# A deeper ring for the streamed halves of a mixture-of-experts combine stage, paid for with single buffers for its two smaller inputs

## The chip, the cores and the metric

The program runs on all 8 cores of one Trainium2 chip. Every core does the whole layer for one of the 8 batch elements (4096 tokens of width 1024); no core waits for another. The metric is the device time of the slowest core, in microseconds.

## The reference, cut to what matters

The layer adds to its input an S4 block and a feed-forward mixture of experts, both computed from the layer-normed input. What the change touches is the second half of the feed-forward part:

```python
h1 = jnp.einsum('td,edi->tei', xf, We1) + be1
h3 = jnp.einsum('td,edi->tei', xf, We3) + be3
h = jax.nn.silu(h1) * h3
yo = jnp.einsum('tei,eid->ted', h, We2) + be2
y = jnp.einsum('te,ted->td', combine, yo)
z = jax.nn.silu(xf @ ws1 + bs1) * (xf @ ws3 + bs3) @ ws2 + bs2
return (y + z).reshape(shape)
```

There are 16 experts of inner width 512 and a shared expert of inner width 1024. `combine` is the routing weight of each token for each expert. All experts are computed densely for all tokens.

## The kernel before, in words

The kernel is written by engine, in phases p0 to p7, with hand-placed semaphores. Each engine's instructions run in the order in which the phases emit them; the order between engines is set by `wait_ge` on semaphores alone. Phases p0 to p5 do the layer norm, the gate, the S4 block and the first half of the experts; p5 leaves silu(h1) in the DRAM tensor `dS` and h3 in `dH`, both bf16 with the inner index as rows and the tokens as columns. `dP` holds the S4 block's output, `dCMBT` the routing weights as 16 rows of 4096 tokens.

Phase p6 (`emit_p6`) is the second half. All second-layer weights stay in SBUF: 16 tiles `w2a[e]`, `ws2b` for the shared expert, and `bep` for the biases. They are loaded at the phase's start by GpSimd DMAs that cast from float32 (L1501, L1505, L1508). The tokens are cut in 16 tiles of 256 (`ts` = 0 to 15), and for each tile the loop runs over 17 steps: e = 0 to 15 for the experts, e = 16 for the shared expert, which is twice as wide. In one step:

- SyncE's queue loads the step's part of `dS` into `sstr[e % 2]` and of `dH` into `hstr[e % 2]` (L1543), 256 KB each, 512 KB each for e = 16. Before it issues them it waits until TensorE has finished the step that used these buffers last, two steps earlier (L1536); across a tile boundary both e = 0 and e = 1 wait for step 16 of the tile before.
- VectorE adds the bias and multiplies the two parts, four instructions of 128x256 (L1613; eight for e = 16), then multiplies all by the routing weights from `cmb6` (L1619; not for e = 16).
- TensorE multiplies the result by the step's weights into a half of PSUM, 32 matmuls of 128x256 (L1595; 64 for e = 16).

After step 16 VectorE adds the bias and the S4 output `abuf` and writes `mtile` (L1628), eight instructions; it does this in its own order before it begins the products of the next tile. GpSimd stores `mtile` to `dM` (L1645). TensorE's bias matmuls of the next tile (L1583) go to the other half of PSUM.

The routing weights of a tile are a load of their own, `cm6load` (L1550): one row of 256 tokens for each of 16 experts, read with a partition stride of 0, so that each of the 128 partitions reads the same 8 KB: 1 MB in pieces of 512 bytes. `cmb6` and `abuf` are double-buffered. SyncE's order in the loop body for tile ts is: all loads of tile ts+1 (`she_load`), then `abuf_load(ts + 2)` (L1559), then `cm6load(ts + 2)`. Since the last step's load of `she_load(ts + 1)` waits for step 14 of tile ts+1, the two small loads of tile ts+2 are issued in the last third of tile ts+1, just ahead of the first loads of tile ts+2.

Phase p7 transposes `dM` back, adds the input and writes the output.

Of the kernel before, what the change touches and what calls it, by code (L numbers as in the profile page):

```python
# [9 lines left out]
BF16 = mybir.dt.bfloat16  # L10
# [72 lines left out]
def ap(t, off, dims):  # L83
    return bass.AP(t, int(off), [[int(a), int(b)] for a, b in dims])
# [1378 lines left out]
def emit_p6(cx):  # L1463
    nc, block, I, D = cx.nc, cx.block, cx.I, cx.D
    sd, sg, sa, cv, ca, ct = cx.sd, cx.sg, cx.sa, cx.cv, cx.ca, cx.ct
# [6 lines left out]
    with p6:  # L1472
        S6 = lambda nm, shp, dt=F32: p6.enter_context(nc.sbuf_tensor(nm, shp, dt))
        w2a = [S6(f"p6_w2{e}", [128, 4096], BF16) for e in range(16)]
        ws2b = S6("p6_ws2", [128, 8192], BF16)
        bep = S6("p6_bep", [128, 1024], BF16)
        hstr = [S6(f"p6_h{j}", [128, 2048], BF16) for j in range(2)]
        sstr = [S6(f"p6_s{j}", [128, 2048], BF16) for j in range(2)]
        abuf = [S6(f"p6_a{j}", [128, 2048], BF16) for j in range(2)]
        cmb6 = [S6(f"p6_cmb{j}", [128, 4096], BF16) for j in range(2)]  # L1480
        mtile = S6("p6_m", [128, 2048], BF16)

        sw6 = cx.newsem("p6w")
        sal = [cx.newsem(f"p6a{j}") for j in range(2)]
        smo = cx.newsem("p6mo")
        scm6 = [cx.newsem(f"p6cm{j}") for j in range(2)]

        @block.vector
        def _(v):
# [21 lines left out]
        NTS = 16  # L1511
# [9 lines left out]
        she = [cx.newsem(f"p6he{j}") for j in range(2)]  # L1521

        def she_cnt(ts, e):
            par = e % 2
            return 32 * (ts * (9 if par == 0 else 8) + e // 2 + 1)

        def she_load(g, ts):
            for e in range(17):
                if e >= 2:
                    tsP, eP = ts, e - 2  # L1530
                elif ts > 0:
                    tsP, eP = ts - 1, 16
                else:
                    tsP = None
                if tsP is not None:
                    g.wait_ge(ct.h, mm_ct(tsP, eP))  # L1536
                    g.wait_ge(she[e % 2].h, she_cnt(ts, e) - 32)
                nic = 8 if e == 16 else 4
                irow = 128 * 64 if e == 16 else e * 512
                for dn, buf in (("dS", sstr[e % 2]), ("dH", hstr[e % 2])):  # L1540
                    src = ap(D[dn], irow * L + ts * 256, [(L, 128), (128 * L, nic), (1, 256)])
                    dst = ap(buf, 0, [(2048, 128), (256, nic), (1, 256)])
                    g.dma_start(out=dst, in_=src).then_inc(she[e % 2].h, 16)  # L1543
                    she[e % 2].val += 16

        def cm6load(g, ts):
            if ts >= 2:
                g.wait_ge(cv.h, prod_cv(ts - 2, 15))
            src = ap(D["dCMBT"], ts * 256, [(0, 128), (L, 16), (1, 256)])
            g.dma_start(out=ap(cmb6[ts % 2], 0, [(4096, 128), (256, 16), (1, 256)]),  # L1550
                        in_=src).then_inc(scm6[ts % 2].h, 16)
            scm6[ts % 2].val += 16

        def abuf_load(g, ts):
            if ts >= 2:
                g.wait_ge(cv.h, evac_cv(ts - 2))
            src = ap(D["dP"], ts * 256, [(L, 128), (128 * L, 8), (1, 256)])
            dst = ap(abuf[ts % 2], 0, [(2048, 128), (256, 8), (1, 256)])
            g.dma_start(out=dst, in_=src).then_inc(sal[ts % 2].h, 16)  # L1559
            sal[ts % 2].val += 16  # L1560

        @block.sync
        def _(sync):
            quiesce(cx, sync, snap)
            abuf_load(sync, 0)
            abuf_load(sync, 1)
            cm6load(sync, 0)
            cm6load(sync, 1)
            she_load(sync, 0)

        for ts in range(NTS):
            @block.tensor
            def _(t):
                if ts == 0:
                    quiesce(cx, t, snap)
                    t.wait_ge(sw6.h, sw6.val)
                    t.wait_ge(cv.h, cv_bz)
                if ts > 1:
                    t.wait_ge(cv.h, evac_cv(ts - 2))
                boff = (ts % 2) * 2048  # L1580
                for dc in range(8):
                    og = PS[:, boff + dc * 256:boff + dc * 256 + 256]
                    t.matmul(og, bep[:, dc * 128:dc * 128 + 128],  # L1583
                             cx.cmbT[:, ts * 256:ts * 256 + 256],
                             start=(dc % 2 == 0), stop=False)
                for e in range(17):
                    t.wait_ge(cv.h, prod_cv(ts, e))
                    nic = 8 if e == 16 else 4
                    buf = hstr[e % 2]
# [12 lines left out]
            def _(v):  # L1602
                vo, vw = mkvo(cx, v)
                for e in range(17):
                    v.wait_ge(she[e % 2].h, she_cnt(ts, e))
                    if e == 0:
                        v.wait_ge(scm6[ts % 2].h, 16 * (ts // 2 + 1))
                    nic = 8 if e == 16 else 4
                    for ic in range(nic):
                        bcol = (cx.sm["be3_t"][:, e * 4 + ic:e * 4 + ic + 1] if e < 16  # L1610
                                else cx.sm["bs3_t"][:, ic:ic + 1])
                        sl = slice(ic * 256, ic * 256 + 256)
                        vw(); vo(v.scalar_tensor_tensor(hstr[e % 2][:, sl], hstr[e % 2][:, sl],  # L1613
                                                        bcol[:, 0:1], sstr[e % 2][:, sl],
                                                        ALU.add, ALU.mult))
                    if e < 16:
                        hv = ap(hstr[e % 2], 0, [(2048, 128), (256, 4), (1, 256)])
                        cmv = ap(cmb6[ts % 2], e * 256, [(4096, 128), (0, 4), (1, 256)])
# [3 lines left out]
                v.wait_ge(sal[ts % 2].h, 16 * (ts // 2 + 1))  # L1622
                if ts > 0:
                    v.wait_ge(smo.h, 16 * ts)
                boff = (ts % 2) * 2048
                for dc in range(8):
                    og = PS[:, boff + dc * 256:boff + dc * 256 + 256]
                    vw(); vo(v.scalar_tensor_tensor(mtile[:, dc * 256:dc * 256 + 256], og,  # L1628
                                                    cx.sm["bs2_t"][:, dc:dc + 1],
                                                    abuf[ts % 2][:, dc * 256:dc * 256 + 256],  # L1630
                                                    ALU.add, ALU.add))
# [147 lines left out]
```

## Time and profile before

| | us |
|---|---|
| median of 2 timed runs | 11503.02 |
| lowest and highest of them | 11441.53, 11564.52 |
| the profiled execution, its own time | 11420.11 |
| its span (slowest core, core 2) | 11418.6 |
| first matmul of phase p6 to its last, core 2 | 8759.3 to 11220.1 |

The profile has one execution. Its views are: a page with shares for each engine; the chain of waits, which follows the work that ended last back to what released it; timelines of an engine or a DMA queue; and windows, which give for a stretch the busy time of each engine, the granted clock of TensorE (1.00 is full speed), the share of the 16 DMA engines and the bytes moved. PE is TensorE, DVE VectorE, POOL GpSimd, SPq the queue on which SyncE issues DMAs. Times are from the span's start.

### The profile page before, as it was taken

How to read it: one execution, taken by the hardware profiler on the slowest of the kernel's cores; microseconds unless marked ns; L12 is line 12 of the kernel's file. 1: busy time of each engine (PE TensorE's matmuls, PEld its weight loads, DVE VectorE, ACT ScalarE, POOL GpSimd, SP SyncE). 2: the span in 40 equal slices, each digit the busy share in tenths (PEclk: the TensorE clock that was granted, in tenths of full speed). 3: DMA queues.
4: the chain of work that ended last, by engine and by line, in shares of the span. 5: the costliest groups of instructions: out<-in, count | busy, mean ns of one | idle time of the engine just before them, and what ended most of it. 6: DMA issues, size and time to landing. Idle time of an engine off the chain costs nothing.

```text
span 11418.6 us, 88364 instructions; the slowest of 8 cores (11167.6 to 11418.6 us)
## 1 busy us (share of the span) xinstructions
PE 4944.3 (43%) x26540; PEld 2771.3 (24%) x26752; DVE 4287.9 (38%) x6820; ACT 2338.6 (20%) x3389; POOL 1803.2 (16%) x3112
## 2 busy tenths in 40 slices
PE   0100097535563553656463333332432655555452
PEld 0000043212221221222121111111111444444341
DVE  6245600433433333333325555554441333333332
ACT  1021033223232232323233333332110000000000
POOL 1000022222222222222222222220000000000000
PEclk9755598767676776767675555555665777777775
DMA  4401232111121221212111111111006333333337
GB/s 137 100 14 27 39 86 73 49 38 51 47 55 36 51 51 30 60 42 55 30 46 27 27 27 27 27 27 39 27 22 100 79 77 74 70 72 76 71 71 170
DMA packets 753737, 637.20 MB, mean 56 GB/s; under 512 B 241553, under 2 KB 653585, under 8 KB 752226
## 3 DMA queue, kind: packets, MB, share of 16 engines
q0 software_dynamic: 173488, 345.61, 12.5%
q1 hardware_dynamic: 475810, 259.72, 10.2%
q10 hardware_dynamic: 103968, 26.22, 1.4%
q8 instruction: 219, 3.59, 0.1%
q14 instruction: 252, 2.06, 0.1%
HBM read 398.38 MB, written 267.52 MB: 58 GB/s over the span
## 4 chain that ended last, share of the span: by engine, by line
PE 32%; DVE 27%; DMA 16%; ACT 9%; issue 7%; POOL 3%; another core or an unknown queue 2%; SPq 1%; DVEq 1%; ACTq 1%; POOLq 0%
PE PS L1407 9%; PE PS L1412 8%; DMA p_h<-dH 8%; PE PS L1595 8%; POOL dKLOC L963 3%; DVE p_h L1613 3%; PE PS L539 2%; DMA dH<-p_h 2%; DMA dKLOC<-p_xbuf 2%; PE PS L1303 2%; ACT L1118 1%; ACT L549 1%; PE PS L1072 1%; DVEq L188 1%
## 5 line engine op out<-in xcount | busy, mean ns | idle before, releaser
L1407 PE MATMUL PS<-xnF,p_w 128*128 128x512 bf16 x4488 | 1163.2, 402 | 1122.2 <-ACT p_h L1435 1054.4
L1595 PE MATMUL PS<-p_h,p_w 128*128 128x256 bf16 x8192 | 1218.3, 325 | 952.6 <-DVE p_h L1619 952.6
L1595 PEld LDWEIGHTS PS<-p_h,p_w 128*128 128x128 bf16 x8192 | 942.4, 116 | 1228.6 <-issue 985.1
L562 DVE TENSOR_TENSOR p_tw<-p_gbuf,s_t1r 128x512 bf16<-128x512 bf16 x128 | 54.4, 425 | 2870.7 <-ACT p_gbuf L550 2870.7
L1412 PE MATMUL PS<-xnF,p_w 128*128 128x512 bf16 x4537 | 1125.3, 391 | 4.4 <-issue 0.4
L1613 DVE SCALAR_TENSOR_TENSOR p_h<-p_h,sb_be_t,p_s 128x256 bf16<-128x256 bf16 x1024 | 495.8, 484 | 1509.8 <-DMA p_h<-dH 1422.9
L1407 PEld LDWEIGHTS PS<-xnF,p_w 128*128 128x128 bf16 x4608 | 470.8, 102 | 1714.2 <-issue 1283.4
L963 POOL DMA_DIRECT2D dKLOC<-p_xbuf x1024 | 599.8, 768 | 1794.1 <-ACT p_xbuf L553 1779.4
L539 PE MATMUL PS<-p_grb,s_s2wr 128*128 128x256 bf16 x256 | 74.9, 395 | 1324.9 <-DVE p_gib L567 1324.9
L1098 PE MATMUL PS<-s_i1a,p_ybuf 128*128 128x256 bf16 x512 | 208.2, 407 | 1012.2 <-DVE p_ybuf L1170 1012.2
L1412 PEld LDWEIGHTS PS<-xnF,p_w 128*128 128x128 bf16 x4608 | 463.4, 101 | 586.5 <-issue 140.6
L1432 ACT ACTIVATE p_s<-PS,sb_be_t 128x512 bf16<-128x512 f32 x512 | 351.9, 687 | 1214.2 <-DMA dH<-p_h 641.7
L1446 POOL DMA_DIRECT2D dS<-p_s x576 | 317.1, 551 | 1454.3 <-ACT p_h L1435 1421.8
L1053 POOL DMA_DIRECT2D p_k<-dKLOC x512 | 314.0, 620 | 1101.2 <-DVE p_tw L1180 1037.4
L1303 PE MATMUL PS<-p_yg,p_wo 128*128 128x512 bf16 x1003 | 262.3, 425 | 462.0 <-DVE p_yg L1275 457.2
L1435 ACT ACTIVATE p_h<-PS 128x512 bf16<-128x512 f32 x576 | 343.5, 596 | 508.1 <-PE PS L1412 508.1
L1645 POOL DMA_DIRECT2D dM<-p_m x16 | 14.2, 890 | 2637.2 <-DVE p_m L1628 2012.4
L539 PEld LDWEIGHTS PS<-p_grb,s_s2wr 128*128 128x128 bf16 x256 | 17.5, 104 | 1381.9 <-issue 1381.9
L1098 PEld LDWEIGHTS PS<-s_i1a,p_ybuf 128*128 128x128 bf16 x512 | 70.2, 137 | 1089.0 <-issue 1064.4
L1449 POOL DMA_DIRECT2D dH<-p_h x576 | 316.7, 550 | 32.2 <-issue 27.0
L1151 DVE TENSOR_TENSOR p_tw<-p_gbuf,s_t1r 128x512 bf16<-128x512 bf16 x128 | 54.4, 425 | 677.5 <-ACT p_gbuf L1119 677.5
L549 ACT ACT_TABLE_LOAD x128 | 164.2, 1283 | 691.2 <-DMA dKLOC<-p_xbuf 651.7
(254 smaller groups left out, 7984.4 us busy)
## 6 DMA issues: line engine op xcount, KB each, us to landing
dS<-p_s POOLq DMA_DIRECT2D x576, 128.0 KB, 2.5
dH<-p_h POOLq DMA_DIRECT2D x576, 128.0 KB, 2.6
p_s<-dS SPq DMA_DIRECT2D x256, 256.0 KB, 3.0
p_h<-dH SPq DMA_DIRECT2D x256, 256.0 KB, 3.3
p_w<-we POOLq DMA_DIRECT2D x48, 1024.0 KB, 17.6
p_x<-x SPq DMA_DIRECT2D x64, 512.0 KB, 5.7
dKLOC<-p_xbuf POOLq DMA_DIRECT2D x1024, 32.0 KB, 2.0
p_k<-dKLOC POOLq DMA_DIRECT2D x512, 64.0 KB, 2.3
```

Of the source, the lines that this page charges most:

```text
L539: ins = t.matmul(XB[xbank][:, sl * 256:sl * 256 + 256], cst[cname][:], src[:, sl * 256:sl * 256 + 256], start=(role == "start" and sl == 0 ...
L963: g.dma_start(out=dst, in_=src).then_inc(sgk.h, 16)
L1053: g.dma_start(out=dst, in_=src).then_inc(skb[bt % 2].h, 16)
L1303: ins = t.matmul(bank, wo[:, hc * 2048 + oc * 128: hc * 2048 + oc * 128 + 128], ygb[:, hc * 512:hc * 512 + 512], start=(hc == 0), stop=(hc ...
L1407: ins = t.matmul(b1, w1b[u % 2][:, dc * 512 + ic * 128: dc * 512 + ic * 128 + 128], cx.xnF[:, dc * L + ts * 512: dc * L + ts * 512 + 512], ...
L1412: ins = t.matmul(b3, w3b[u % 2][:, dc * 512 + ic * 128: dc * 512 + ic * 128 + 128], cx.xnF[:, dc * L + ts * 512: dc * L + ts * 512 + 512], ...
L1432: ins = s.activation(s1b[n % 2][:], b1, AF.Silu, bias=bcol, scale=1.0)
L1435: ins = s.activation(h3b[n % 2][:], b3, AF.Copy)
L1446: g.dma_start(out=dst, in_=s1b[n % 2][:]).then_inc(sht[n % 2].h, 16)
L1449: g.dma_start(out=dst, in_=h3b[n % 2][:]).then_inc(sht[n % 2].h, 16)
L1595: ins = t.matmul(og, wsrc[:, ic * H + dc * 128: ic * H + dc * 128 + 128], buf[:, ic * 256:ic * 256 + 256], start=False, stop=(e == 16 and ...
L1613: vw(); vo(v.scalar_tensor_tensor(hstr[e % 2][:, sl], hstr[e % 2][:, sl], bcol[:, 0:1], sstr[e % 2][:, sl], ALU.add, ALU.mult))
```

## The change

Inside p6, `hstr` and `sstr` get four buffers each in place of two, with four semaphores. Step e now uses buffer e % 4, and its load waits for the step four before it. Across a tile boundary e = 0 waits for step 16 of the tile before, e = 1, 2 and 3 for steps 13, 14 and 15. To make room, `abuf` and `cmb6` fall from two buffers to one. Their loads for tile ts+1 therefore wait for the last use in tile ts: `cm6load(ts + 1)` for the product of expert 15 of tile ts, `abuf_load(ts + 1)` for the evacuation of tile ts. SyncE's order in the body for tile ts becomes `cm6load(ts + 1)`, `she_load(ts + 1)`, `abuf_load(ts + 1)`. At the start one `abuf` and one `cmb6` load are issued, where there were two of each. The arithmetic, the sizes of all transfers and the order on VectorE and TensorE stay.

```diff
-        hstr = [S6(f"p6_h{j}", [128, 2048], BF16) for j in range(2)]
-        sstr = [S6(f"p6_s{j}", [128, 2048], BF16) for j in range(2)]
-        abuf = [S6(f"p6_a{j}", [128, 2048], BF16) for j in range(2)]
-        cmb6 = [S6(f"p6_cmb{j}", [128, 4096], BF16) for j in range(2)]
+        hstr = [S6(f"p6_h{j}", [128, 2048], BF16) for j in range(4)]
+        sstr = [S6(f"p6_s{j}", [128, 2048], BF16) for j in range(4)]
+        abuf = S6("p6_a", [128, 2048], BF16)
+        cmb6 = S6("p6_cmb", [128, 4096], BF16)
...
         def she_load(g, ts):
             for e in range(17):
-                if e >= 2:
-                    tsP, eP = ts, e - 2
+                if e >= 4:
+                    tsP, eP = ts, e - 4
                 elif ts > 0:
-                    tsP, eP = ts - 1, 16
+                    tsP, eP = ts - 1, (16 if e % 4 == 0 else 12 + e % 4)
                 else:
                     tsP = None
                 if tsP is not None:
                     g.wait_ge(ct.h, mm_ct(tsP, eP))
-                    g.wait_ge(she[e % 2].h, she_cnt(ts, e) - 32)
+                    g.wait_ge(she[e % 4].h, she_cnt(ts, e) - 32)
...
         def cm6load(g, ts):
-            if ts >= 2:
-                g.wait_ge(cv.h, prod_cv(ts - 2, 15))
+            if ts >= 1:
+                g.wait_ge(cv.h, prod_cv(ts - 1, 15))
...
         def abuf_load(g, ts):
-            if ts >= 2:
-                g.wait_ge(cv.h, evac_cv(ts - 2))
+            if ts >= 1:
+                g.wait_ge(cv.h, evac_cv(ts - 1))
...
             quiesce(cx, sync, snap)
             abuf_load(sync, 0)
-            abuf_load(sync, 1)
             cm6load(sync, 0)
-            cm6load(sync, 1)
             she_load(sync, 0)
...
             def _(sync):
                 if ts + 1 < NTS:
+                    cm6load(sync, ts + 1)
                     she_load(sync, ts + 1)
-                if ts + 2 < NTS:
-                    abuf_load(sync, ts + 2)
-                    cm6load(sync, ts + 2)
+                    abuf_load(sync, ts + 1)
```

## Rows read from the trace of the kernel before

**Rows 1.** The page: head, engines' busy time, shares of the chain by line.

```profile
span 11418.6 us, 88364 instructions; the slowest of 8 cores (11167.6 to 11418.6 us)
PE 4944.3 (43%) x26540; PEld 2771.3 (24%) x26752; DVE 4287.9 (38%) x6820; ACT 2338.6 (20%) x3389; POOL 1803.2 (16%) x3112
PE PS L1407 9%; PE PS L1412 8%; DMA p_h<-dH 8%; PE PS L1595 8%; POOL dKLOC L963 3%; DVE p_h L1613 3%; PE PS L539 2%; DMA dH<-p_h 2%; DMA dKLOC<-p_xbuf 2%; PE PS L1303 2%; ACT L1118 1%; ACT L549 1%; PE PS L1072 1%; DVEq L188 1%
```

**Rows 2.** Chain of waits, core 2, two steps: start us, us, what.

```profile
10128.34 6.26 PE PS L1595 x32
10134.71 0.36 SPq L1543
10135.11 3.84 DMA p_h<-dH
...
10142.31 6.10 PE PS L1595 x32
```

**Rows 3.** Timeline of DVE, core 2, same steps: start us, us, engine line op.

```profile
10125.15 2.25 DVE L1613 SCALAR_TENSOR_TENSOR p_h<-p_h,sb_be_t,p_s 128x256 bf16<-128x256 bf16 x4 [31.97 <-DMA p_h<-dH]
10127.50 0.69 DVE L1619 TENSOR_TENSOR p_h<-p_h,p_cmb 128x1024 bf16<-128x1024 bf16 x1
10128.30 2.25 DVE L1613 SCALAR_TENSOR_TENSOR p_h<-p_h,sb_be_t,p_s 128x256 bf16<-128x256 bf16 x4
```

**Rows 4.** Timeline of PE, core 2, the same boundary.

```profile
10063.83 7.22 PE L1595 MATMUL PS<-p_h,p_w 128*128 128x256 bf16 x64 [3.38 <-DVE p_h L1619]
10079.86 8.40 PE L1595 MATMUL PS<-p_h,p_ws 128*128 128x256 bf16 x64 [8.81 <-DVE p_h L1613]
10088.11 1.04 PE L1583 MATMUL PS<-cmbT,p_bep 128*128 128x256 bf16 x8
10128.34 9.74 PE L1595 MATMUL PS<-p_h,p_w 128*128 128x256 bf16 x64 [39.20 <-DVE p_h L1619]
```

**Rows 5.** Timeline of SyncE's DMA queue, core 2, the same boundary.

```profile
10068.01 0.58 SPq L1543 DMA_DIRECT2D p_h<-dH  x1
10068.70 2.65 SPq L1559 DMA_DIRECT2D p_a<-dP  x1
10071.45 1.69 SPq L1550 DMA_DIRECT2D p_cmb<-dCMBT  x1
10088.41 0.36 SPq L1543 DMA_DIRECT2D p_s<-dS  x1
10088.82 10.41 SPq L1543 DMA_DIRECT2D p_h<-dH  x1
```

**Rows 6.** Chain of waits, core 2: loads after the last step of a tile.

```profile
9009.07 25.05 DMA p_h<-dH
...
11060.54 35.74 DMA p_h<-dH
...
11210.41 9.73 PE PS L1595 x64
```

**Rows 7.** Timeline of PE, core 2: phase p6's start and its first boundary.

```profile
8759.34 1.86 PE L1583 MATMUL PS<-cmbT,p_bep 128*128 128x256 bf16 x8 [205.94 <-DMA p_bep<-be]
...
8881.86 1.04 PE L1583 MATMUL PS<-cmbT,p_bep 128*128 128x256 bf16 x8
8890.17 10.27 PE L1595 MATMUL PS<-p_h,p_w 128*128 128x256 bf16 x64 [7.27 <-DVE p_h L1619]
```

**Rows 8.** Line L1550 on core 2, from issue to landing.

```profile
L1550 SPq DMA_DIRECT2D p_cmb<-dCMBT x16: 1446/1506/8319, 8559.4 to 11041.5; - x16
...
DMA to landing us min/median/max: 39.7/50.1/107.3
```

**Rows 9.** Lines L1550 and L1595 on core 6.

```profile
DMA to landing us min/median/max: 31.6/35.0/123.5
...
L1595 PE MATMUL PS<-p_h,p_w x8192: 269/273/421, 8870.1 to 11135.4; 128*128 128x256 bf16 x200
L1595 PE MATMUL PS<-p_h,p_ws x1024: 272/273/421, 8975.6 to 11152.6; 128*128 128x256 bf16 x171
```

**Rows 10.** Windows, core 2: engines' busy us (x instructions), PEclk, DMA share, GB/s.

```profile
1537.00:1648.00 111.00, 103.92 (x475) 47.15 (x482) 0.00 (x0) 37.73 (x58) 33.48 (x61) 0.99 0.34 89
5082.00:5146.00 64.00, 58.60 (x220) 24.26 (x223) 25.32 (x14) 16.72 (x27) 15.82 (x28) 0.80 0.43 95
8620.00:8660.00 40.00, 0.00 (x0) 0.00 (x0) 0.00 (x0) 0.00 (x0) 0.00 (x0) 0.50 0.85 81
8691.00:8747.00 56.00, 0.00 (x0) 0.00 (x0) 2.63 (x5) 0.00 (x0) 0.00 (x0) 0.50 1.05 166
10068.00:10074.00 6.00, 3.05 (x28) 2.48 (x26) 0.00 (x0) 0.00 (x0) 0.00 (x0) 1.00 0.87 235
10076.00:10103.00 27.00, 9.28 (x72) 7.59 (x72) 6.96 (x15) 0.00 (x0) 0.89 (x1) 0.69 0.30 25
10249.00:10407.00 158.00, 81.03 (x546) 62.57 (x544) 49.80 (x96) 0.00 (x0) 0.89 (x1) 0.71 0.34 74
```

More of the change, by code:

```diff
@@ L1476, in emit_p6 @@
         bep = S6("p6_bep", [128, 1024], BF16)
-        hstr = [S6(f"p6_h{j}", [128, 2048], BF16) for j in range(2)]
-        sstr = [S6(f"p6_s{j}", [128, 2048], BF16) for j in range(2)]
-        abuf = [S6(f"p6_a{j}", [128, 2048], BF16) for j in range(2)]
-        cmb6 = [S6(f"p6_cmb{j}", [128, 4096], BF16) for j in range(2)]
+        hstr = [S6(f"p6_h{j}", [128, 2048], BF16) for j in range(4)]
+        sstr = [S6(f"p6_s{j}", [128, 2048], BF16) for j in range(4)]
+        abuf = S6("p6_a", [128, 2048], BF16)
+        cmb6 = S6("p6_cmb", [128, 4096], BF16)
         mtile = S6("p6_m", [128, 2048], BF16)
         sw6 = cx.newsem("p6w")
-        sal = [cx.newsem(f"p6a{j}") for j in range(2)]
+        sal = cx.newsem("p6a")
         smo = cx.newsem("p6mo")
-        scm6 = [cx.newsem(f"p6cm{j}") for j in range(2)]
+        scm6 = cx.newsem("p6cm")
         @block.vector
@@ L1519, in emit_p6 @@
         evac_cv = lambda ts: cv0 + ts * VV6 + VV6
-        she = [cx.newsem(f"p6he{j}") for j in range(2)]
+        she = [cx.newsem(f"p6he{j}") for j in range(4)]
+        CNT4 = [5, 4, 4, 4]
         def she_cnt(ts, e):
-            par = e % 2
-            return 32 * (ts * (9 if par == 0 else 8) + e // 2 + 1)
+            return 32 * (ts * CNT4[e % 4] + e // 4 + 1)
         def she_load(g, ts):
             for e in range(17):
-                if e >= 2:
-                    tsP, eP = ts, e - 2
+                if e >= 4:
+                    tsP, eP = ts, e - 4
                 elif ts > 0:
-                    tsP, eP = ts - 1, 16
+                    tsP, eP = ts - 1, (16 if e % 4 == 0 else 12 + e % 4)
                 else:
@@ L1536, in she_load @@
                     g.wait_ge(ct.h, mm_ct(tsP, eP))
[L1537 removed]
+                    g.wait_ge(she[e % 4].h, she_cnt(ts, e) - 32)
                 nic = 8 if e == 16 else 4
                 irow = 128 * 64 if e == 16 else e * 512
[L1540 removed]
+                for dn, buf in (("dS", sstr[e % 4]), ("dH", hstr[e % 4])):
                     src = ap(D[dn], irow * L + ts * 256, [(L, 128), (128 * L, nic), (1, 256)])
                     dst = ap(buf, 0, [(2048, 128), (256, nic), (1, 256)])
[L1543 to L1544 removed]
+                    g.dma_start(out=dst, in_=src).then_inc(she[e % 4].h, 16)
+                    she[e % 4].val += 16
         def cm6load(g, ts):
[L1547 to L1548 removed]
+            if ts >= 1:
+                g.wait_ge(cv.h, prod_cv(ts - 1, 15))
             src = ap(D["dCMBT"], ts * 256, [(0, 128), (L, 16), (1, 256)])
[L1550 to L1552 removed]
+            g.dma_start(out=ap(cmb6, 0, [(4096, 128), (256, 16), (1, 256)]),
+                        in_=src).then_inc(scm6.h, 16)
+            scm6.val += 16
         def abuf_load(g, ts):
[L1555 to L1556 removed]
+            if ts >= 1:
+                g.wait_ge(cv.h, evac_cv(ts - 1))
             src = ap(D["dP"], ts * 256, [(L, 128), (128 * L, 8), (1, 256)])
[L1558 to L1560 removed]
+            dst = ap(abuf, 0, [(2048, 128), (256, 8), (1, 256)])
+            g.dma_start(out=dst, in_=src).then_inc(sal.h, 16)
+            sal.val += 16
         @block.sync
@@ L1588, in _ @@
                     nic = 8 if e == 16 else 4
-                    buf = hstr[e % 2]
+                    buf = hstr[e % 4]
                     wsrc = ws2b if e == 16 else w2a[e]
@@ L1604, in _ @@
                 for e in range(17):
-                    v.wait_ge(she[e % 2].h, she_cnt(ts, e))
+                    v.wait_ge(she[e % 4].h, she_cnt(ts, e))
                     if e == 0:
-                        v.wait_ge(scm6[ts % 2].h, 16 * (ts // 2 + 1))
+                        v.wait_ge(scm6.h, 16 * (ts + 1))
                     nic = 8 if e == 16 else 4
@@ L1629, in _ @@
                                                     cx.sm["bs2_t"][:, dc:dc + 1],
-                                                    abuf[ts % 2][:, dc * 256:dc * 256 + 256],
+                                                    abuf[:, dc * 256:dc * 256 + 256],
                                                     ALU.add, ALU.add))
```

10 lines of the change are left out of this document (5 added, 5 removed).

## The prediction, written before the changed kernel was run

> **What bounds the kernel now.** I read the page first: no engine is busy for half of the span, and the chain of the work that ended last gives 8% of it to matmuls of L1595 and 8% to loads of `p_h` [rows 1]. Both belong to phase p6, the only one that the change touches, so everything else is kept as it is. On core 2 the phase's matmuls run from 8759.3 to 11220.1 (the last row of [rows 6]), 2461 us for 16 tiles; one of them, from one boundary to the next, is the 158 us of the last window of [rows 10].
>
> Inside a tile I followed the chain of waits. One step in two shows the same loop [rows 2]: 32 matmuls 6.26 us, 0.36 us of issue, a load of 3.84 us, VectorE, and matmuls again at 10142.31, 14.0 us after the previous pair began. So two steps pass in 14.0 us, 7.0 us for each. The loop is load plus VectorE plus matmuls of one buffer, and with two buffers two steps share it. What the reader is to see is that no engine is full: VectorE needs 3.15 us for a step (start 10125.15 to start 10128.30 in [rows 3]), and 64 matmuls that run on without a break take 7.22 us at the full clock [rows 4], 3.61 us for a step. The same 64 take 9.74 us after a pause, because the first 32 of them take about 6.3 us: in the idle stretch the granted clock is at 0.50 (1.2 GHz), and it comes back to 2.4 GHz only once the matmuls have run for a while.
>
> Then the boundary between tiles. There the chain has a long load: 14 boundaries from 25.05 to 39.99 us, the first and the last of them shown [rows 6], in sum 467.1 us, 33.4 us each. TensorE's own gap is about 39 us [rows 4]. The queue shows why [rows 5]: the routing weights of `cm6load` are issued at 10071.45, behind the last step's load, and the first load of the next tile comes behind them at 10088.41; its second half's issue alone takes 10.41 us, since the queue is full. The routing load takes 50.1 us from issue to landing (median, [rows 8]), though it has no more bytes than the last step's load: while it alone is in flight 25 GB/s move, against 235 GB/s just before [rows 10]. It is slow by itself, and what stands behind it in the queue waits. The one boundary that has no such load in front of it costs 7.27 us [rows 7].
>
> **The change part by part.**
>
> *Four buffers in place of two.* The load for step e is issued when step e-4 is done, three steps ahead of its use. Its own loop, 0.1 + 0.4 + 3.8 us of load and 3.2 us of VectorE, 7.5 us, fits in three steps of any length that TensorE can reach (3 x 3.61 = 10.8 us). VectorE needs 3.15 us for a step, under 3.61, so TensorE sets the pace. The DMA engines must bring 512 KB in a step of 4 us, 131 GB/s; the window shows 235 GB/s [rows 10], so they are no bound. What a step costs depends on the clock alone. At full clock it is 3.61 us. For the other end I take a stretch of continuous matmuls in an earlier phase where the granted clock is 0.80: 220 matmuls in 58.60 us are 266 ns each against 219 ns (475 in 103.92) at 0.99 [rows 10]; scaled by the clocks, 3.61 x 0.99 / 0.80 = 4.47 us. I choose 4.0 us between the two, since the earlier phases show continuous stretches of both sorts. The first step after a pause stays at 6.5 us, and step 16 with its 64 matmuls takes 8.0. A tile's matmuls are then 6.5 + 15 x 4.0 + 8.0 = 74.5 us.
>
> *The routing load at the boundary.* It moves in the program, but not in effect. It must wait for the product of expert 15, whose load is released by step 11. Counted from the end of step 12, that load is released at -4.0, lands at about -0.2 and is multiplied by +3.0; there the routing load is issued. Step 16 ends at 3 x 4.0 + 8.0 = 20.0, so it starts 17 us ahead of the first load of the next tile. Before it was 10088.41 - 10071.45 = 17.0 us [rows 5]. Ahead of it in the queue are the same two transfers as before, the last step's and `abuf`'s. The gap at a boundary thus stays what it was: 33.4 us to the landing, 0.5 us of issue and 3.4 us of VectorE, 37.3 us. Behind the waiting routing load stand only the loads of the next tile; the first of these would have to wait for step 16 anyway. What changes is that steps 1, 2 and 3 are now in the queue too, and land together with step 0.
>
> Two things differ. There are 15 such boundaries now and not 14: the first, 7.27 us before [rows 7], becomes one of 37.3. And with single buffers the routing load is no longer only in the way, the products also need it; but it lands ahead of the loads behind it, so this adds nothing. If that cover were gone, VectorE would wait for it at the same place.
>
> *`abuf` with one buffer.* It is issued behind the last step's load, about a step after the end of step 12, and needed 20 us later; 1.5 MB at 235 GB/s take 6.4 us. It costs nothing; late by more than 13 us it would add what it is late.
>
> *The start.* One routing load and one `abuf` load less, and the loads of two steps more, before the weights are in. During the second routing load the weights come at a total of 81 GB/s for 40 us, later at 166 [rows 10]: the loss is 40 x (1 - 81/166) = 20 us. The extra 0.5 MB net cost 3 us. I take a gain of 17 us, between 0 and 20.
>
> *The sum*, on core 2: the first tile 1.9 (the bias matmuls, [rows 7]) + 74.5 = 76.4, then 15 x (37.3 + 74.5) = 15 x 111.8 = 1677, together 1753 us against 2461, 708 less; with the start 725 less. The profiled execution then takes 11420 - 725 = 10695 us. Its time is 83 us under the median of the two timed runs; against that median the forecast is 11503 - 725 = 10778, say 10780 us.
>
> The Trainium skill bears on the clock. The trace shows continuous matmuls at a granted clock of 0.99 and at 0.80 [rows 10], in one core, at different times. The skill (TensorE: Matmul & The Clock Gate, Part 1: The HAM clock gate) says that with three or more cores of a die in dense matmuls a limiter takes the clock to 13/16, and that an all-core kernel should be budgeted so. The row at 0.80 agrees, the row at 0.99 does not; the rule's result is the second rival below.
>
> **The rivals.**
>
> *A shorter gap.* On core 6 the same load lands in 35.0 us (median, [rows 9]) against 50.1 on core 2. If the gap on the slow cores falls by the difference to 18.3 us, and the clock is full, a boundary costs 22.2 and a tile 6.5 + 54.2 + 7.2 = 67.9: 69.8 + 15 x 90.1 = 1421 us. Then the core with the latest start decides, core 6, with 2283 us now (8870.1 to 11152.9) in a span of 11341.2: 11341 - 862 - 17 = 10462, by the median 10545 us. For it speaks that the same transfer with the same bytes is so much shorter on another core; against it, that core 2 has the longer one as a median over the whole phase, and the change gives it no reason to shrink.
>
> *The clock stays at 0.80.* With 4.47 us for a step (the scaled value above) a tile is 6.5 + 67.1 + 8.9 = 82.5, and 84.4 + 15 x 119.8 = 1881 us, 580 less, 597 with the start: 10906 us. For it: TensorE will be busy for 74 of 112 us on all cores, where it is 81 of 158 now.
>
> *The routing load gets slower.* It is half of a tile's time now and will be more often in flight in two cores at once. With the longest gap seen, about 41 us, and the clock at 0.80, a tile is 44.9 + 82.5 = 127.4 and the sum 1995: 466 less, 11037 us.
>
> *Not faster.* The gain of 725 us is gone if a boundary costs 725 / 15 = 48 us more, that is if the routing load needs about 98 us and not 50. The longest landing is 107.3 us [rows 8], at the start beside the weights, where two routing loads stand behind each other. At 107 us each the sum would be 15 x 57 = 855 us worse: 11633 us. It decides from 98 us on. Against it: nothing but the weights' start shows such a landing, and the loads of the next tile are behind it, not beside it.
>
> **How the numbers follow.** The forecast case, pace between 3.61 and 4.47 us and a gap near 37 us, gets 0.5; the shorter gap 0.15; the low clock 0.2; the slower routing load 0.1; not faster 0.05, of which I give 0.03 to slower and 0.02 to within 2%. The other cases all end below 11273 us, 2% under the median, but a mixture of a slow routing load and steps that do not reach TensorE's pace could reach 11,300, so 0.06 is within 2%, 0.03 slower, 0.91 faster. 2% is about what a measurement of this kernel can tell from no change. The range goes from the shorter gap, a little under 10545, to the slower routing load: 10500 to 11040 us.
>
> **What would show it.** Right: in a tile, 17 steps of matmuls without a gap of over 1 us, a tile of about 112 us, VectorE busy about 50 of them; one gap of 35 to 42 us at each of 15 boundaries; landing of the routing load near 50 us; first matmul near 8742. Wrong: gaps inside a tile that end with a load (then the loads share bandwidth and the pace is theirs), steps of over 4.5 us at full clock, boundaries far from 37 us, or a first matmul that does not move. The forecast fails most likely by the gap, which is a third of a tile and depends on how the cores stand to each other.

## The result, and the profile after

The changed kernel is faster: 10684.42 us (median of 11 runs, 10592.08 to 10743.75) against 11413.0 us for the kernel before (10 runs, 11317.1 to 11564.52), a ratio of 0.9373 with a 95% interval from 0.9326 to 0.9419. The forecast was 10780 us against a median of 11503, a ratio of 0.937. The profiled execution took 10609.44 us. In some executions one die runs at a lower clock throughout and takes some per cent longer; the ratios given with an interval leave these out, and as e9's profile is one of them, the table has its other die, cores 0 to 3.

The page of the changed kernel, its head and the shares of the chain by line (now L1593 is the matmul of a step, L1611 and L1617 the products, L1581 the bias matmul; L1543, L1550 and L1559 are as before). They answer to [rows 1].

```profile
span 10607.9 us, 88574 instructions; the slowest of 8 cores (10452.6 to 10607.9 us)
PE PS L1407 9%; PE PS L1412 9%; PE PS L1593 8%; DMA p_h<-dH 7%; POOL dKLOC L963 3%; DMA dH<-p_h 2%; PE PS L539 2%; DMA dKLOC<-p_xbuf 2%; ACT L1118 2%; ACT L549 2%; PE PS L1072 1%; DMA dP<-p_at 1%; DVEq L188 1%; DVE p_h L1611 1%
```

TensorE's timeline on the slowest core, core 1, over one tile and its boundary (start us, us, engine line op, idle before and its releaser). It answers to [rows 4].

```profile
9578.32 57.79 PE L1593 MATMUL PS<-p_h,p_w 128*128 128x256 bf16 x512 [39.20 <-DVE p_h L1617]
9638.02 7.15 PE L1593 MATMUL PS<-p_h,p_ws 128*128 128x256 bf16 x64 [1.91 <-DVE p_h L1611]
9645.00 1.04 PE L1581 MATMUL PS<-cmbT,p_bep 128*128 128x256 bf16 x8
9690.42 9.80 PE L1593 MATMUL PS<-p_h,p_w 128*128 128x256 bf16 x70 [44.38 <-DVE p_h L1617]
```

The 16 expert steps are now one run of 512 matmuls without a gap, 3.6 us for a step, where [rows 4] has pairs of steps with stops of 3.4 us. One stop is left, 44.38 us here. It is longer than it was: over the 15 boundaries its median by core is 32 to 44 us, where the kernel before had 21 to 23 us on six cores and 38 us on cores 2 and 3.

SyncE's DMA queue on the same core at that boundary answers to [rows 5]. The second fence is from the chain of waits (start us, us, what): the second half of step 0's load, from issue to landing.

```profile
9626.16 0.58 SPq L1543 DMA_DIRECT2D p_h<-dH  x1
9626.84 2.30 SPq L1559 DMA_DIRECT2D p_a<-dP  x1
9631.03 0.36 SPq L1550 DMA_DIRECT2D p_cmb<-dCMBT  x1
9645.30 1.36 SPq L1543 DMA_DIRECT2D p_s<-dS  x1
9646.72 12.81 SPq L1543 DMA_DIRECT2D p_h<-dH  x1
```

```profile
9646.72 40.27 DMA p_h<-dH
```

Windows of the same core (columns as in [rows 10]): the tile's steps, and the stop.

```profile
9578.00:9626.00 48.00, 47.68 (x421) 42.03 (x422) 35.41 (x69) 0.00 (x0) 0.00 (x0) 0.96 0.50 137
9647.00:9688.00 41.00, 0.00 (x0) 0.00 (x0) 3.23 (x8) 0.00 (x0) 0.89 (x1) 0.54 0.51 68
```

Of the 811 us between the two profiled spans (11418.6 on core 2 and 10607.9 on core 1), 720 are the stage: 2461 us of matmuls on the slowest core before, 1741 after (8680.0 to 10420.9). Another 79 lie ahead of its first matmul, 8759.3 and 8680.0; of them 18 are the wait for the weights, 205.7 and 188.1 us. The other 61, and 12 us behind the last matmul, come from phases that the change does not touch. They move from run to run: in the profiles of this study the stage's first matmul stands anywhere from 8608 to 8903. The experiments are therefore read by the stage's own time, from the first bias matmul to the last matmul. By core it was 2253 to 2461 us before and is 1597 to 1741 after.

### The profile page after: what moved, and what is told of

Same layout as the page of the kernel before. It is cut to its first block, busy times and chain, and to the rows that moved or that the text cites. A ratio compares the mean times of both kernels' runs of the same rounds, so it can differ in the third digit from the quotient of the medians.

```text
span 10607.9 us, 88574 instructions; the slowest of 8 cores (10452.6 to 10607.9 us)
## 1 busy us (share of the span) xinstructions
PE 4553.8 (43%) x26752; PEld 2604.8 (25%) x26752; DVE 4288.7 (40%) x6820; ACT 2337.7 (22%) x3389; POOL 1803.1 (17%) x3112
## 4 chain that ended last, share of the span: by engine, by line
PE 32%; DVE 26%; DMA 16%; ACT 10%; issue 7%; POOL 4%; another core or an unknown queue 2%; SPq 1%; DVEq 1%; ACTq 1%; POOLq 0%
PE PS L1407 9%; PE PS L1412 9%; PE PS L1593 8%; DMA p_h<-dH 7%; POOL dKLOC L963 3%; DMA dH<-p_h 2%; PE PS L539 2%; DMA dKLOC<-p_xbuf 2%; ACT L1118 2%; ACT L549 2%; PE PS L1072 1%; DMA dP<-p_at 1%; DVEq L188 1%; DVE p_h L1611 1%
## 5 line engine op out<-in xcount | busy, mean ns | idle before, releaser
L1407 PE MATMUL PS<-xnF,p_w 128*128 128x512 bf16 x4608 | 1146.1, 394 | 1127.1 <-ACT p_h L1435 1072.1
L1593 PE MATMUL PS<-p_h,p_w 128*128 128x256 bf16 x8192 | 929.7, 278 | 642.6 <-DVE p_h L1617 642.6
L1412 PE MATMUL PS<-xnF,p_w 128*128 128x512 bf16 x4608 | 1097.3, 381 | 0.0
L1593 PEld LDWEIGHTS PS<-p_h,p_w 128*128 128x128 bf16 x8192 | 816.0, 100 | 756.4 <-issue 646.6
L1611 DVE SCALAR_TENSOR_TENSOR p_h<-p_h,sb_be_t,p_s 128x256 bf16<-128x256 bf16 x1024 | 496.0, 484 | 908.0 <-DMA p_h<-dH 812.8
```

The source lines that it names most:

```text
L1407: ins = t.matmul(b1, w1b[u % 2][:, dc * 512 + ic * 128: dc * 512 + ic * 128 + 128], cx.xnF[:, dc * L + ts * 512: dc * L + ts * 512 + 512], ...
L1412: ins = t.matmul(b3, w3b[u % 2][:, dc * 512 + ic * 128: dc * 512 + ic * 128 + 128], cx.xnF[:, dc * L + ts * 512: dc * L + ts * 512 + 512], ...
L1611: vw(); vo(v.scalar_tensor_tensor(hstr[e % 4][:, sl], hstr[e % 4][:, sl], bcol[:, 0:1], sstr[e % 4][:, sl], ALU.add, ALU.mult))
```

## The experiments

The table gives the stage's time over the eight cores, TensorE's stop ahead of a tile's first step (each core's median over the 15 boundaries), and the routing load's time from issue to landing (each core's median).

| kernel | stage us | stop at a boundary us | routing load us |
|---|---|---|---|
| before | 2253 to 2461 | 21 to 23, cores 2 and 3 38 | 35 to 37, cores 2 and 3 50 and 51 |
| b1, before, load of distinct addresses | 2018 to 2044 | 7 to 8 | 9 to 10 |
| e3, two buffers, small inputs single | 2472 to 2593 | 36 to 44 | 50 to 56 |
| e4, three buffers | 1697 to 1809 | 28 to 36 | 39 to 48 |
| after, four buffers | 1597 to 1741 | 32 to 44 | 40 to 52 |
| e7, routing load on ScalarE's queue | 1655 to 1751 | 32 to 44 | 42 to 53 |
| e2, distinct addresses | 1183 to 1224 | 7 | 7 to 9 |
| e1, no reload | 1184 to 1346 | 7 | none |
| e5, contiguous 8 KB | 1188 to 1287 | 7 | 6 to 8 |
| e8, contiguous in DRAM, rows padded in SBUF | 1184 to 1254 | 7 | 7 to 9 |
| e9, rows 8704 bytes apart | 1182 to 1197 | 7 | 7 to 9 |
| e6, 16 copies | 1182 to 1190 | 7 | not in the trace |
| e10, ring runs on | 1057 to 1135 | none | 6 to 8 |

### Is the stop at a boundary the routing load?

e1_no_reload leaves the 15 later loads out:

```diff
                 if ts + 1 < NTS:
-                    cm6load(sync, ts + 1)
                     she_load(sync, ts + 1)
```

> The changed kernel, with the routing weights loaded once, for tile 0, and used for all tiles; the 15 later routing loads are left out, so the routing weights of tiles 1 to 15 are wrong ones. In the changed kernel TensorE stands still for about 44 us at each of 15 tile boundaries. Theory (the routing load stands in the queue in front of the next tile's first load): the stop falls to what the boundary without such a load showed in the kernel before, 7 to 9 us, so 15 x 35 = 525 us less, span near 10080 us. Rival (the stop is made by the four steps' loads issued together and by the store of the tile's output, which share the DMA engines): the stop stays above 25 us, span above 10350 us.

Measured: the slowest core's span is 10221.9 us, the stage 1184 to 1346, and the 15 stops are 7.2 to 7.3 us (medians). The rival, that the four steps' loads or the store of `mtile` make the stop, falls: both are still there. The span is 140 us longer than the theory said, although the stops are as forecast. On core 2, the slowest, the reason is the clock: its stage takes 1346 us and that of core 0 1188. (Core 0's own span, 10177.9 us, is long for another reason: its stage starts at 8801.5, some 120 us later than in the changed kernel.) Windows of 200 us of this kernel, on core 2 and then on core 0:

```profile
9400.00:9600.00 200.00, 184.19 (x1418) 152.81 (x1417) 120.41 (x232) 0.00 (x0) 1.77 (x2) 0.82 0.45 126
...
9400.00:9600.00 200.00, 181.46 (x1601) 159.19 (x1602) 138.66 (x267) 0.00 (x0) 2.30 (x3) 0.95 0.51 144
```

TensorE is busy in 92% and 91% of the time on both, but core 2 is granted 0.82 and does 1418 matmuls, core 0 is granted 0.95 and does 1601.

### Why is that load slow?

The first idea was that all 128 partitions of a core read the same 8 KB. e2_distinct reads the same bytes, in the same pieces, from places of their own:

```diff
-            src = ap(D["dCMBT"], ts * 256, [(0, 128), (L, 16), (1, 256)])
+            src = ap(D["dH"], ts * 256, [(L, 128), (128 * L, 16), (1, 256)])
```

> The changed kernel; the routing load reads the same number of bytes in the same 512-byte pieces, at the same place in the queue, but each partition reads addresses of its own (from dH), so the routing weights are wrong ones. Theory (slow since all 128 partitions of a core read the same 8 KB): it lands in 6 to 9 us as the other loads of 1 MB do, the stop at a boundary falls to 7 to 10 us, span near 10090 us. Rival (slow for its form, 2048 small pieces with 16 rows for each partition): landing stays near 50 us and the stop near 44 us, span near 10610 us.

It lands in 7 to 9 us and the stop is 7.3 us, as on core 4:

```profile
9580.11 7.15 PE L1593 MATMUL PS<-p_h,p_ws 128*128 128x256 bf16 x64 [0.58 <-DVE p_h L1611]
9587.09 1.04 PE L1581 MATMUL PS<-cmbT,p_bep 128*128 128x256 bf16 x8
9595.46 58.27 PE L1593 MATMUL PS<-p_h,p_w 128*128 128x256 bf16 x512 [7.33 <-DVE p_h L1617]
```

So neither the form of the transfer nor its place in the queue is slow, but the addresses. e5_tile_major puts the 16 rows of a tile side by side in DRAM:

```diff
-            src = ap(D["dCMBT"], ts * 256, [(0, 128), (L, 16), (1, 256)])
+            src = ap(D["dCMBT"], ts * 4096, [(0, 128), (1, 4096)])
```

> The changed kernel; the routing weights lie in DRAM tile by tile, so the routing load reads one contiguous run of 8 KB for each partition, the same 8 KB for all 128. Theory (the limit is the rate at which one small region of DRAM is read): landing stays at 35 to 55 us, the stop at a boundary near 40 us, matmuls of the stage 1600 to 1740 us. Rival (the limit is the time for each 512-byte piece): with pieces 16 times longer it lands in under 15 us, the stop falls to about 8 us, and the stage takes 1190 to 1230 us.

The theory falls. All partitions still read the same 8 KB, and the load lands in 6 to 8 us. e6_replicas16, prepared for the theory, could show nothing more:

> As e5_tile_major, but with 16 copies of the routing weights in DRAM, each read by 8 partitions. Theory (rate of one region): 16 regions give 16 times the rate, it lands in 6 to 12 us, the stop at a boundary is 7 to 10 us, the stage takes 1190 to 1230 us where the clock stays full and 1300 to 1350 us where it is granted at 0.8, and the span is 10100 to 10350 us with the full computation. Rival (e5 already fast): no difference to e5.

Its stage takes 1182 to 1190 us, as on the best cores of e5 (1188 and 1189). e5 changed two things, the length of a piece and the distance of the rows. The next two kernels were meant to change one each. e8_contig_small keeps the contiguous 8 KB and pads the rows in SBUF (258 elements and not 256), in order to have pieces of 512 bytes again:

> As e5_tile_major (contiguous 8 KB in DRAM, the same for all partitions), but the destination rows are padded, so that the load is cut in pieces of 512 bytes again. Theory A (many short reads of one small region are slow, whatever its layout): landing back at 35 to 55 us, the stop at a boundary 36 to 46 us, the stage 1600 to 1740 us. Theory B (the 16 rows 8192 bytes apart are what makes the repeated reads slow, since they fall together in DRAM): landing 7 to 12 us, the stop near 8 us, the stage 1180 to 1290 us.

e9_row_pad keeps the 16 rows and the pieces of 512 bytes and lets the rows in DRAM lie 8704 bytes apart:

```diff
-    D["dCMBT"] = nc.dram_tensor("dCMBT", [E, L], BF16)
+    D["dCMBT"] = nc.dram_tensor("dCMBT", [E, L + 256], BF16)
...
-            src = ap(D["dCMBT"], ts * 256, [(0, 128), (L, 16), (1, 256)])
+            src = ap(D["dCMBT"], ts * 256, [(0, 128), (L + 256, 16), (1, 256)])
```

> The changed kernel with the routing weights in 16 rows as before, but the rows 8704 bytes apart and not 8192; pieces of 512 bytes. Theory A (many short reads of one small region): landing stays at 35 to 55 us, the stage 1600 to 1740 us. Theory B (the distance of 8192 bytes): landing 7 to 15 us, the stop near 8 us, the stage 1180 to 1290 us.

The padding in SBUF did not do what e8 was built for. The pages of e5 and of e8 (the slowest core of each) count the same packets:

```profile
DMA packets 723032, 637.19 MB, mean 62 GB/s; under 512 B 241553, under 2 KB 620817, under 8 KB 719490
```

```profile
DMA packets 723032, 637.19 MB, mean 63 GB/s; under 512 B 241553, under 2 KB 620817, under 8 KB 719490
```

The changed kernel and e9 have 753736. The difference is 30704, and 16 loads of 128 packets of 8 KB in place of 2048 of 512 bytes would save 30720. So e8 still moved pieces of 8 KB; it repeats e5 and decides nothing between the theories. e9 does, for it has small pieces, read 128 times, and only the distance is another. It bears out theory B. From issue to landing in e8 (core 2) and then in e9 (core 0), where core 1 of the changed kernel has the third row:

```profile
DMA to landing us min/median/max: 6.1/7.4/9.2
```

```profile
DMA to landing us min/median/max: 5.5/7.2/10.3
```

```profile
DMA to landing us min/median/max: 46.5/51.7/56.0
```

A padding of 512 bytes in each row, with everything else as it was, makes the load 7 times faster. What is slow is to read 16 pieces 8192 bytes apart over and over. The loads of `dS`, `dH` and of e2 also have rows 8192 bytes apart, but each piece is read once, and they are fast. Which part of the memory's addressing does this was not seen; that the pieces fall together in it is argued from the layouts, not shown. Whether contiguous pieces of 512 bytes, read over and over, are fast was not tested.

e7_act_queue moves the load to ScalarE's queue, which has nothing else to do in this stage:

> The changed kernel with the routing load issued from ScalarE's queue, so that the next tile's first loads do not stand behind it. Theory (with a single buffer the products need the routing weights at the same moment, so the queue is not the only gate): the load of the first step lands early but VectorE waits for the routing load instead; the stop stays at 36 to 46 us and the stage within 60 us of the changed kernel's 1600 to 1740 us. Rival (the queue's order is the whole cost): the stop falls under 25 us.

The stage takes 1655 to 1751 us, as the theory said, and the stop is 32 to 44 us (medians), on four cores under the theory's 36. But its reason is not what the trace shows. SyncE's queue on core 3, which no longer holds the routing load:

```profile
9572.62 0.36 SPq L1543 DMA_DIRECT2D p_s<-dS  x1
9573.03 13.01 SPq L1543 DMA_DIRECT2D p_h<-dH  x1
9586.19 9.84 SPq L1543 DMA_DIRECT2D p_s<-dS  x1
```

The second half of the tile's first load still takes 13.01 us to issue. The theory had it landing early; it lands at 9614.33, 4.3 us behind the routing load (9610.04), and VectorE, idle for 37 us, goes on only then. So the loads of another queue are held up while the slow reads run. It also shows that the long issue, which the prediction put down to a full queue, does not need a routing load in that queue. A queue of its own was no help against this load.

### Do the two costs add?

b1_before_distinct is the kernel before with e2's edit:

> The kernel before (two ring buffers, double-buffered small inputs), its routing load reading the same bytes at addresses of its own for each partition, so the routing weights are wrong ones. Theory (the two costs of the kernel before add up: the pace of two buffers inside a tile, and the routing load at a boundary): the stop at a boundary falls from 39 to 8 us, 14 x 31 = 430 us less on a core that had 39, and the stage takes 16 x 126 = 2020 us, all cores alike. Rival (the routing load also slows the steps inside a tile): the stage takes under 1950 us.

The stage takes 2018 to 2044 us where 2020 was worked out. With fast loads the pace of two buffers is left alone, and it is what was worked out. With this the four corners are known: two buffers and the slow load 2253 to 2461, two and a fast one 2018 to 2044, four and the slow one 1597 to 1741, four and a fast one 1183 to 1224 (e2). The ring is worth 650 to 720 us with the slow load, and about 830 without it. So the two costs do not simply add: in the mean over the cores the slow load costs 297 us of the stage with two buffers (2324 and 2027) and 473 us with four (1668 and 1195). With four there is one more boundary, and on most cores the load lands later; what sets that is taken up with e3 and at the end.

### The other half of the change, and the ring's depth

e3_two_single keeps two ring buffers and takes over the single `abuf` and `cmb6` and the order of the loads:

```diff
-        hstr = [S6(f"p6_h{j}", [128, 2048], BF16) for j in range(4)]
-        sstr = [S6(f"p6_s{j}", [128, 2048], BF16) for j in range(4)]
+        hstr = [S6(f"p6_h{j}", [128, 2048], BF16) for j in range(2)]
+        sstr = [S6(f"p6_s{j}", [128, 2048], BF16) for j in range(2)]
```

> One half of the change alone: abuf and cmb6 single-buffered, their loads in the changed order, but two ring buffers as before. Theory (the single buffers and the new order cost only the first boundary, 30 us, and give back about 20 us at the start): matmuls of the stage take 2461 us plus 30, span within 40 us of that of the kernel before run beside it. Rival (the single-buffered routing load is a new wait of its own, hidden in the changed kernel by the shorter tile): the stop at each boundary is longer than in the kernel before by 5 us or more, the stage takes 2570 us or more.

By its numbers the rival is met on two cores: the stage takes 2593 and 2585 us on cores 0 and 1. Its mark for the stop is met on more cores: by median the stop is 36 to 44 us, where six cores of the kernel before had 21 to 23. One boundary of core 0 has 44.20 us where the kernel before has 27.80 us there, the second fence:

```profile
9595.49 9.65 PE L1593 MATMUL PS<-p_h,p_w 128*128 128x256 bf16 x64 [44.20 <-DVE p_h L1617]
```

```profile
9553.34 9.32 PE L1595 MATMUL PS<-p_h,p_w 128*128 128x256 bf16 x64 [27.80 <-DVE p_h L1619]
```

But the landing changed too, from 36 to 55 us on core 0. Where it is alike, the theory holds: cores 6 and 7 of e3 have 50 and 51 us and a stage of 2492 and 2472; cores 2 and 3 of the kernel before have 50 and 51 us and 2461 and 2443. That is 30 us more, the first boundary. So the single buffers are not a wait of their own; what grew is the landing. It goes with the distance to the neighbouring core (last section). Whether the single buffers help to bring that about is open.

e4_three has a ring of three:

```diff
-                if e >= 4:
-                    tsP, eP = ts, e - 4
+                if e >= 3:
+                    tsP, eP = ts, e - 3
```

> The changed kernel with a ring of three buffers in place of four. Theory (a buffer's own loop of issue, load, VectorE and matmuls is 0.1 + 0.4 + 3.8 + 3.2 + 3.6 = 11.1 us, and three of TensorE's steps at full clock are 10.8): the pace is 3.6 to 3.8 us for a step, at most 16 x 0.2 = 3 us a tile and 50 us in all slower than four buffers, span 10600 to 10660 us. Rival (loads in flight slow each other, and depth gives more than the loop's sum says): the pace is over 4.1 us, span above 10740 us.

The stage takes 1697 to 1809 us; over the eight cores it is 95 us more in the mean than with four, where the loop's sum said 50 at most. Even this hides a part: the tiles' matmuls take 10.3 us more each (78.6 and 68.3 in the mean), 164 us for 16, and the stops, which the ring's depth does not make, happen to be shorter (33.6 and 38.2 us from the end of step 16), 69 us less for 15. A step takes 4.0 us in the tile below (16 of them in 64.7) and 4.07 to 4.31 us by core over all tiles, with the slow first step included; six of the eight cores are past the rival's 4.1. (The span, 10851 us, is past the rival's mark too, but on that core the stage also began some 185 us later than on the slowest core of the changed kernel.) The chain of waits on core 3 (start us, us, what):

```profile
9589.43 7.16 PE PS L1594 x64
9596.70 0.36 SPq L1544
9597.10 5.07 DMA p_h<-dH
...
9605.53 3.67 PE PS L1594 x32
```

The sum's form is right and one term is not: this load takes 5.07 us, not 3.8. Over the kernel the median of its second half is 4.1 us on core 3, where the kernel before has 3.3 on core 2; a third step's load is now in flight beside the others. A loop is then 8.9 us from the end of the matmuls to the next start, plus 3.7, or 12.6; three steps share it, 4.2 us each. With a load of 3.8 it would be 11.3, or 3.8 for a step. Four buffers have room for this.

### A version that beats both

e10_run_on is e5 with two edits: the ring is indexed by the step's number in the whole stage, so the first loads of a tile do not wait for step 16 of the last; and VectorE does the products of steps 0 and 1 of the next tile before the evacuation.

```diff
-                if e >= 4:
-                    tsP, eP = ts, e - 4
-                elif ts > 0:
-                    tsP, eP = ts - 1, (16 if e % 4 == 0 else 12 + e % 4)
+                if gi(ts, e) >= 4:        # gi = ts * 17 + e
+                    g.wait_ge(ct.h, ct0 + gi(ts, e) - 3)
```

> e5_tile_major with the ring of four running on across tiles (a buffer by the step's number in the whole stage) and with the products of the next tile's steps 0 and 1 ahead of the evacuation on VectorE. e5 has 15 stops of 7.4 us, 111 us in all, and 64 to 68 us of matmuls a tile at full clock. Theory (the stops are the first load and the evacuation in front of the first product, and nothing else): the stops fall below 1 us, the stage takes 16 x 66 = 1056 to 1090 us at full clock; where the clock is granted at 0.8 for the whole stage it takes 16 x 76 = 1220 us. Rival (without stops the clock is held at 0.8 on all cores, which takes back most of the gain): the stage takes 1200 us or more on all cores, no faster than e5's 1188 to 1287.

Measured: 9999.63 us (median of 4 runs), and a ratio of 0.8733 to the kernel before, with a 95% interval from 0.8661 to 0.8805. The stage takes 1057 to 1135 us. TensorE on core 1 at a boundary:

```profile
9307.55 7.15 PE L1628 MATMUL PS<-p_h,p_ws 128*128 128x256 bf16 x64 [0.51 <-DVE p_h L1582]
9314.53 1.04 PE L1616 MATMUL PS<-cmbT,p_bep 128*128 128x256 bf16 x8
9315.40 7.15 PE L1628 MATMUL PS<-p_h,p_w 128*128 128x256 bf16 x64
9323.18 49.07 PE L1628 MATMUL PS<-p_h,p_w 128*128 128x256 bf16 x448 [0.63 <-DVE p_h L1587]
```

The stop of 44 us is gone and the theory holds. The rival, no faster than e5 on any core, falls: on core 0 a window of 200 us with TensorE busy for 193 has a granted clock of 1.00. But the low clock is there on other cores, and cores 2 to 5 take 1109 to 1135 us, over the 1090 of the full clock. Core 2:

```profile
9400.00:9600.00 200.00, 200.00 (x1534) 166.06 (x1533) 130.76 (x253) 0.00 (x0) 2.66 (x3) 0.82 0.53 156
```

e11_tile_major_timed runs e5 once more with the time taken:

> The kernel e5_tile_major once more, timed: its stage took 1188 to 1287 us where the changed kernel's took 1597 to 1741, about 430 us less, so against the kernel before (11413 us median over ten runs; the changed kernel 10684) its time should be 10684 - 430 = 10250 us, a ratio of 0.89 to 0.905.

Its median is 10130.42 us (4 runs) against 11425.89 us for the kernel before beside it, a ratio of 0.887 with no interval taken, a little better than expected. The profiled executions of the changed kernel and of this one are 503 us apart (10609.44 and 10106.65), the medians 554, the changed kernel's from other runs. So a new layout of one small tensor is worth some 500 us or more on top of the ring; of this the stage accounts for 467 us on the slowest cores (1741 and 1274).

## Why the prediction was right

**The reading of the kernel before** held. The two costs that it named, the pace of two buffers and the routing load in front of a tile's first load, are there: b1 takes the second away and leaves the first, e1 and e2 take it away from the changed kernel. The size of the second was read on core 2 as if it were fixed. The same trace shows it moving: its load landed in 40 to 45 us at tiles 2 to 6 and in 48 to 54 from tile 7 on, and in 35 to 37 us in the median on the six cores other than 2 and 3.

**Four buffers.** TensorE sets the pace inside a tile, as stated. The size was off: 512 matmuls take 57.79 us, 3.61 us for a step with the first included, and e10 has 448 in 49.07, 3.51. The forecast had 4.0 for a step, between a full and a low clock, and 6.5 for the first. The granted clock inside the tile was 0.96. Together with step 16 this tile takes 66.9 us on core 1 and not 74.5.

The rival in which the clock stays low did not happen on the cores that decide, but it did for much of the stage on cores 4 and 5, whose tiles take 67 to 79 and 66 to 77 us. Two tiles of core 4 (columns as in [rows 10]):

```profile
8781.40:8860.70 79.30, 76.86 (x578) 62.92 (x579) 43.25 (x83) 0.00 (x0) 0.00 (x0) 0.81 0.45 104
10249.20:10316.00 66.80, 65.51 (x576) 57.25 (x575) 43.18 (x83) 0.00 (x0) 0.00 (x0) 0.96 0.43 119
```

It cost nothing in the end because these cores have the short stop. As an estimate, core 4's tiles (73.2 us in the mean) with core 1's gaps (43.7) would make a stage of 16 x 73.2 + 15 x 43.7 = 1827 us, 86 more than core 1's. The limiter of which the Trainium skill tells (TensorE: Matmul & The Clock Gate, Part 1: The HAM clock gate) takes a whole die to 13/16 of the clock, 0.81. The first row has that number. That it holds a whole die does not agree: e1 shows cores 2 and 3 near 0.8 and cores 0 and 1 of the same die at 0.92 to 0.97, at the same load, and e10 has core 2 at 0.82 and core 0 at 1.00 in the same window.

**The boundary.** The load's place came out nearly as worked out: the routing load is issued 14.3 us ahead of step 0's load (9631.03 and 9645.30), not 17, since product 15 was ready 5.4 us after step 12 and not 3.0. The size was off the other way: 45.3 us from the end of step 16 to the next matmul on core 1, not 37.3. Of the 8 us, 6.9 are the landing of step 0's load, 40.27 us where the mean of the 14 was 33.4, and 1.1 its issue, 1.6 us after step 16 and not 0.5; VectorE's 3.4 us are as forecast. Behind the landing stand the shorter lead, 2.7 us, and a routing load that lands in 51.7 us on this core where the one of the forecast, 50.1 us in the median of core 2, had been faster at the early boundaries. So the term that was mis-sized is the landing of 33.4 us.

**The sum.** On core 1, which decides now, the two errors cancel: 74.5 + 37.3 = 111.8 was the forecast for a tile, 66.9 + 45.3 = 112.2 is what this tile took, and over 15 tiles the mean is 111.6. On core 2, for which the sum was made, they cancel only in part: the stage took 1687 us and not 1753, with tiles of 65.9 us in the mean (138 us less for 16) and gaps of 42.1 (72 more for 15). There is luck in the last step too. The gain of 725 us was taken from a median of two runs, 11503; from the median of ten, 11413, it gives 10688, and 10684 was measured. But the two profiled spans lie 811 us apart. That the ratio came out at 0.937 is owed to these as much as to the mechanism.

**`abuf`** costs nothing, as stated. One small wait was not foreseen: step 16 starts 1.91 us late, since its load of 1 MB is issued only after step 12 and its second half needs 6.95 us.

**The start.** 17 us were forecast on core 2, between 0 and 20. The wait for the weights fell from 205.9 to 183.8 us there, 22 us, and by 30 us in the mean over the eight cores, with one profile of each kernel. The 18 us between the two slowest cores compare core 2 with core 1, and are near 17 by chance.

**The first boundary**, 7.27 us before, now has a stop like the others: 44 us on core 2, where 37 were forecast. In e3 it is the 30 us.

**The rival of a shorter gap** did not happen. Cores 4 and 5 have a landing of 40 and 41 us and gaps of 32 and 31 us, and these too are longer than they were there, 22 and 23. On no core did the gap shrink.

**The rival of a slower routing load** was half right: it had a gap of 44.9 us together with a clock of 0.80. The gap came on core 0, 44.7 us in the mean, and nearly on core 1, 43.7; on both the routing load went from 36 and 37 us in the median to 51 and 52. The low clock came elsewhere, on cores 4 and 5. **The rival of no gain**, a routing load of 98 us, showed nowhere; the longest median is 56, in e3.

## What to carry to other kernels

When a stage has both a pace and a stop, work out each from its own rows; deepening a ring pays for the pace only, and the stop stays until its own cause is taken away. When a forecast keeps a wait as it is, read that wait on all cores and over the whole stage; in the kernel before it went from 18 to 44 us. Ask of the longest transfer in a chain why it is longer than others of its size: here the slow layout of one small tensor cost 473 us of the stage, where the ring was worth 656 (means over the cores). A forecast that comes out right should still be taken apart by terms, since two of its terms may be wrong in opposite ways.

## What the runs showed of the hardware that was not expected

- A load in which 128 partitions read the same 16 pieces of 512 bytes takes 35 to 56 us (medians) when the pieces are 8192 bytes apart, and 7 to 9 us when they are 8704 bytes apart (e9). As one piece of 8 KB it takes 6 to 9 us (e5, e8). 1 MB moves in all.
- While it runs, loads of another queue are slow: in e7 the second half of the next load takes 13.01 us to issue.
- Its length goes with the neighbouring core (0 with 1, 2 with 3, and so on). Over the 560 slow loads of the kernel before, the changed kernel, e3, e4 and e7, without each core's first two, the landing has a median of 54.9 us when the neighbour issued its own load less than 10 us earlier or later, 50.4 us at 15 to 20, 45.3 us at 25 to 30, and 38.4 us at over 40. The correlation of landing and distance is -0.85; with any other core in the neighbour's place it lies between -0.03 and 0.10. Each core's times count from its own first instruction, so the distances rest on the cores starting together. This fits two neighbours slowing each other's reads; no run changed the distance alone.
- The distance was not planned and differs from profile to profile: at the stage's first matmul cores 0 and 1 are 18 us apart in the kernel before and 6 us in the changed one. How much of the longer stop is owed to the change, and how much to this, is open.
- Under the same load two cores of a die can be granted 0.8 and the other two 0.95 (e1). What decides it stayed open; e10 works TensorE harder and had 0.98 to 1.00 on cores 0 and 7 over windows of 200 us, and 0.91 and 0.93 on cores 5 and 2 over 600 us.
